# Cross attention with 64-dim heads: reciprocals spread as three bf16 rows, the output projection ahead of the next spread

## The reference, cut to what matters

```python
def _L1_xattn_ref(x, context, Wq, Wk, Wv, Wout, bout):
    HEADS, DIM_HEAD = 8, 64
    SCALE = DIM_HEAD ** (-0.5)
    b, n, _ = x.shape                 # 32, 128, 128
    m = context.shape[1]              # 128 (width 96)
    q = (x @ Wq).reshape(b, n, HEADS, DIM_HEAD)
    k = (context @ Wk).reshape(b, m, HEADS, DIM_HEAD)
    v = (context @ Wv).reshape(b, m, HEADS, DIM_HEAD)
    sim = jnp.einsum('bihd,bjhd->bhij', q, k) * SCALE
    attn = jax.nn.softmax(sim, axis=-1)
    out = jnp.einsum('bhij,bjhd->bihd', attn, v).reshape(b, n, HEADS * DIM_HEAD)
    return out @ Wout + bout
...
x = _layernorm(x + _L1_xattn_ref(x, ctx_768, ...), axis=-1)
```

## Time and profile before

| | us |
|---|---|
| median of 3 runs | 3455.29 (3452.86 to 3456.10) |
| the profiled execution | 3453.05 |
| its span in the trace | 3451.3 |
| the stage of the change, about | 1157 to 1449 in the span |
| PE / PEld / DVE / ACT / POOL busy | 80% / 57% / 57% / 40% / 37% |

### The profile page before, as it was taken

How to read it: one execution, slowest core, us unless ns; L and a number is a source line. 1 busy time by engine, 2 the same in 40 slices (tenths; PEclk the granted TensorE clock), 3 DMA queues, 4 the chain that set the end, 5 groups by cost and what they waited for, 6 DMA issues and landing times. The chain is left out here.

```text
span 3451.3 us, 78570 instructions
## 1 busy us (share of the span) xinstructions
PE 2777.9 (80%) x31785; PEld 1976.5 (57%) x31785; DVE 1960.1 (57%) x5133; ACT 1387.4 (40%) x3112; POOL 1272.5 (37%) x1365
## 2 busy tenths in 40 slices
PE   6980466577667699799899996798979999988986
PEld 3550233265443477556699985566456666665665
DVE  5987988406456344366554444464755555544665
ACT  3540455416334455344422222454133434334554
POOL 3440243317221111345323333453743333324555
PEclk9995677659678899899899998898999999998998
DMA  3000000030000000000000000001000000000000
GB/s 99 3 2 2 1 1 1 1 107 1 1 6 1 32 2 2 39 3 3 8 1 1 1 1 1 17 2 42 0 5 2 2 2 2 2 2 8 2 2 25
DMA packets 24454, 37.29 MB, mean 11 GB/s; under 512 B 569, under 2 KB 21185, under 8 KB 23233
## 3 DMA queue, kind: packets, MB, share of 16 engines
q1 hardware_dynamic: 24096, 32.30, 2.9%
HBM read 30.07 MB, written 2.23 MB: 9 GB/s over the span
## 5 line engine op out<-in xcount | busy, mean ns | idle before, releaser
L1193 POOL TENSOR_TENSOR L_attn__qk<-L_attn__turned 128x512 f32<-128x512 f32 x128 | 161.5, 1273 | 352.7 <-DVE L_attn__turned L1302 352.7
L4218 PE MATMUL psum<-L_ffn__e_hT,weights 128*128 128x256 f32 x1024 | 244.4, 382 | 0.0
L777 DVE TENSOR_REDUCE L_xattn__nm<-psum 128x8 bf16<-128x1024 f32 x128 | 156.4, 1224 | 149.4 <-PE psum L970 143.0
L1302 DVE TENSOR_TENSOR L_attn__turned<-psum,weights 128x1024 f32<-128x1024 f32 x128 | 153.4, 1219 | 144.7 <-PE psum L1409 141.7
L4218 PEld LDWEIGHTS psum<-L_ffn__e_hT,weights 128*128 128x128 f32 x1024 | 186.5, 192 | 20.5
L4072 DVE TENSOR_TENSOR L_ffn__e_a<-L_ffn__e_sg,psum 128x512 f32<-128x512 f32 x128 | 87.9, 687 | 176.2 <-ACT L_ffn__e_sg L4064 176.2
L4064 ACT ACTIVATE L_ffn__e_sg<-psum 128x512 f32<-128x512 f32 x128 | 76.5, 598 | 258.4 <-PE psum L4218 258.4
L717 ACT ACTIVATE L_xattn__pT<-psum 128x1024 f32<-128x1024 f32 x128 | 124.0, 1021 | 59.0 <-PE psum L998 59.0
L4231 PEld LDWEIGHTS psum<-weights,L_ffn__e_a 128*128 128x128 f32 x1024 | 134.4, 191 | 7.2 <-DVE L_ffn__e_a L4072 0.7
L1409 PE MATMUL psum<-L_attn__xT,weights 128*128 128x256 f32 x512 | 136.2, 399 | 1.9 <-DVE L_attn__turned L1302 1.2
L4231 PE MATMUL psum<-weights,L_ffn__e_a 128*128 128x128 f32 x1024 | 135.0, 275 | 0.5 <-DVE L_ffn__e_a L4072 0.5
(11 more groups left out here) (677 smaller groups left out, 7613.3 us busy)
## 6 DMA issues: line engine op xcount, KB each, us to landing
L_xattn__toeplitz<-s4d_kernel SPq DMA_DIRECT2D x8, 1024.0 KB, 5.7
weights<-pack SPq DMA_DIRECT2D x1, 3328.0 KB, 10.5
weights<-pack SPq DMA_DIRECT2D x1, 3140.0 KB, 10.5
weights<-pack SPq DMA_DIRECT2D x1, 2370.0 KB, 9.2
out_dram<-X SPq DMA_DIRECT2D x1, 2048.0 KB, 8.7
weights<-pack SPq DMA_DIRECT2D x1, 1732.5 KB, 10.3
ctxT<-ctxT_in SPq DMA_DIRECT2D x1, 1536.0 KB, 22.0
weights<-pack SPq DMA_DIRECT2D x1, 1376.0 KB, 5.5
```

The source lines that it names most:

```text
L777: nc.vector.tensor_reduce(nm[:, n % 2, :].rearrange("p (g c) -> p g c", g=4)[:, 2 * u:2 * u + 2, 0:4], scores[u].rearrange("p g (i q) -> p ...
L1193: nc.gpsimd.tensor_tensor(qk[:, p % 2, u], turned[:, g % 2, :, 0:2 * P], turned[:, g % 2, :, 2 * P:4 * P], ALU.add).then_inc(qk_sb, 1)
L1302: nc.vector.tensor_tensor(turned[:, g % 2], proj[u % 2].unsqueeze(1).to_broadcast([P, 2, 4 * P]), k.w(name + "rope").rearrange("p (t q) -> ...
L4218: last = nc.tensor.matmul(bank[g % 2][:, 256 * c:256 * c + 256], k.w(name + w)[:, o:o + P], hT, start=True, stop=True)
```

## The change

The reciprocal is no longer spread as one f32 row per head but as three bf16 rows that add up to it. The rows of C that `weigh` fills come in groups of 32, and each group holds several copies of its denominators, in rows that repeat every two. `spread2` now selects three of these copies, and DVE makes them different: the first holds the value rounded to bf16, the second the rounded remainder, the third the remainder of that. The columns `part_of_row` say which rows subtract. That takes five more DVE operations, each waiting for the one before, and `parts` has two buffers. PE's four matmuls read bf16 on both sides; the constant is cast to bf16 at the stage's start, and PE waits for that. `project_out(n - 1)` comes before `spread(n)`, behind a new wait for the reciprocal (inv_sb), as the reciprocal reads the bank C that the output is written to.

```diff
-    return (p == D64 * half + 32 * (c // 2) + c % 2).astype(np.float32).reshape(P, -1)
+    first = D64 * half + 32 * (c // 2) + c % 2
+    return ((p == first) | (p == first + 2) | (p == first + 4)).astype(np.float32).reshape(P, -1)
+def part_of_row():
+    part = np.arange(P) % 32 // 2
+    return np.stack([np.where(part == 0, 0.0, -1.0), np.where(part == 2, -1.0, 0.0)], 1).astype(np.float32)
...
                 def inverted(n):
                     dve.wait_ge(den_ps, n + 1)
-                    if n >= 1:
-                        dve.wait_ge(over_ps, n)
-                    nc.vector.reciprocal(rd[:], C[:, 0:P]).then_inc(rd_sb, 1)
+                    nc.vector.reciprocal(rd[:], C[:, 0:P]).then_inc(inv_sb, 1)
+                    dve.wait_ge(inv_sb, n + 1)
+                    nc.vector.tensor_copy(hi[:], rd[:]).then_inc(hi_sb, 1)
+                    dve.wait_ge(hi_sb, n + 1)
+                    nc.vector.scalar_tensor_tensor(out=less_hi[:], in0=hi[:], scalar=not_hi, in1=rd[:], op0=ALU.mult,
+                                                   op1=ALU.add).then_inc(less_hi_sb, 1)
+                    dve.wait_ge(less_hi_sb, n + 1)
+                    nc.vector.tensor_copy(himid[:], less_hi[:]).then_inc(himid_sb, 1)
+                    dve.wait_ge(himid_sb, n + 1)
+                    nc.vector.scalar_tensor_tensor(out=less_mid[:], in0=himid[:], scalar=is_lo, in1=less_hi[:],
+                                                   op0=ALU.mult, op1=ALU.add).then_inc(less_mid_sb, 1)
+                    dve.wait_ge(less_mid_sb, n + 1)
+                    if n >= 2:
+                        dve.wait_ge(over_ps, n - 1)
+                    nc.vector.tensor_copy(parts[:, n % 2, :], less_mid[:]).then_inc(rd_sb, 1)
...
                 dve.wait_ge(k.loaded[stage], 16)
+                nc.vector.tensor_copy(spread16[:], k.w(name + "spread2")).then_inc(spread16_sb, 1)
...
-                        last = nc.tensor.matmul(scores[n % 2][:, 1, P * c:P * c + P], spread2[:, P * c:P * c + P], rd[:],
+                        last = nc.tensor.matmul(scores[n % 2][:, 1, P * c:P * c + P], spread16[:, P * c:P * c + P], parts[:, n % 2, :],
...
                 pe.wait_ge(k.ctx_loaded, 16)
+                pe.wait_ge(spread16_sb, 1)
...
-                    spread(n)
                     if more and n % 2 == 0:
                         project(p + 1, 3)
                     if n >= 1:
+                        pe.wait_ge(inv_sb, n + 1)
                         project_out(n - 1)
+                    spread(n)
                     if n % 2 == 1 and p + 2 <= LAST:
                         turn_x(p + 2)
```

More of the change, by code:

```diff
@@ L230, in host_pack @@
     put(4, n + "spread2", spread2())
+    put(4, n + "part_of_row", part_of_row())
     n = "L1_ffn_"
@@ L1590, in attention64_cross @@
         sums2 = k.w(name + "sums2")
-        spread2 = k.w(name + "spread2")
+        spread16 = sb("spread16", [P, C2 * P], BF16)
+        hi, himid, parts = sb("hi", [P, P], BF16), sb("himid", [P, P], BF16), sb("parts", [P, 2, P], BF16)
+        less_hi, less_mid = sb("less_hi", [P, P]), sb("less_mid", [P, P])
+        not_hi, is_lo = k.w(name + "part_of_row")[:, 0:1], k.w(name + "part_of_row")[:, 1:2]
         scores = [k.psum[:, 4 + 2 * r:6 + 2 * r, :] for r in range(2)]
@@ L1607, in attention64_cross @@
         var_eps, rstd_sb, x_out = event("ln_var_eps"), event("ln_rstd"), event("x_out")
+        inv_sb, hi_sb, less_hi_sb, himid_sb, less_mid_sb, spread16_sb = (
+            event(n) for n in ("inv_sb", "hi_sb", "less_hi_sb", "himid_sb", "less_mid_sb", "spread16_sb"))
         with nc.Block() as block:
```

## The result

In 15 runs each the changed kernel took 3463.36 us in the median (3454.50 to 3465.61) and the kernel before 3455.29 (3450.29 to 3457.37): ratio 1.0023, 95% interval 1.0016 to 1.0030. In a second set (11 and 27 runs) it was 3459.34 against 3455.43, ratio 1.0018 (1.0009 to 1.0027). So the change costs 3 to 10 us, where 2.75 were forecast.

The account below looks back on a forecast made before the run. PE seemed the bound (busy 232.72 of 240 us), but ACT's queue was taken to gate its saving. Terms +1.4, +0.45, -0.2, +0.8 and +0.3 gave +2.75 us: 3458.0, range 3449 to 3466, its own 3453 to 3463.

Parts of the forecast that it names:

- Spread on PE: PE's spread matmuls: 1.00 us falls to 0.30 (bounds 0.22 and 0.39), saving 0.70 a step.
- The split on DVE: Three casts and two scalar_tensor_tensor behind each reciprocal on DVE: 1.50 us, bounds 1.3 and 1.9.
- rival (b): Split on DVE so short that it hides behind the output block: about 3450 us; chance 0.05.
- rival (c): Parts and spread cost more, POOL contention on DVE possible, each step pays: up to 3473, mostly near 3464; chance 0.22.
- The new order: Output before spread: even steps keep 0.08 of 0.93 us because ACT's queue waits, odd steps lose 0.18.
- rival (a): PE's saving carries into the next step, ACT's queue not the gate: -0.75 us a pair, 3445; chance 0.10.
- start: Cast of spread2 at the stage's start, 0.42 us, of which PE sees about 0.3.
- up to L1848 of step 1: Step 0 has no output block, so spread waits for its parts: +0.45 us.
- pairs and late steps: 14 pairs cost +1.4 us; two late steps without x transpose or projections gain 0.1 each.
- behind the last L1848: Last sequence has no cover: spread eviction 1.50 later less the 0.70 of spread, +0.8 us.
- Rival (d): PE, standing 1.3 us more in a pair, loses its clock; price like the slower-parts rival's; chance 0.03.
- The sum: Whole kernel +2.75 us, from a median of 3455.29 to 3458.0; chance 0.60.

Follow-up runs that it names:

- both handovers: Changed kernel with ACT evicting last projection and x before the spread, PE transposing x before waiting for parts: 3439.55 against 3455.43 before, ratio 0.9959.
- second trace: Trace of the changed kernel run again without an edit: median 3459.34 against 3455.43 for the kernel before, ratio 1.0018.
- first trace: First trace of the changed kernel, its execution 3465.61 us; median of that set 3463.36 against 3455.29 for the kernel before, ratio 1.0023.
- the control with the two columns: Kernel before with only the unused part_of_row columns added to the packed weights: median 3454.91, ratio 0.9996 to before.

## Why the prediction was right, and where it was off

**Spread on PE.** Taken at 0.30 us; it takes 0.23 (1402.66 to 1402.89), at the lower bound. The eviction starts 0.43 after its first matmul (0.50 was taken). The Trainium skill, "TensorE: Matmul & The Clock Gate", section "Back-to-back issue gap", gives 81 ns for each matmul of 128 columns in a stream of weight loads and matmuls. Four would take 0.32 us, an estimate from that page; the trace's 0.23 is less.

**The split on DVE.** Taken at 1.50 us from the reciprocal's end; it takes 1.55 (1410.34 to 1411.89). The combining steps were right (0.35), the casts 0.23 instead of 0.21: the line through 256 and 512 columns doesn't reach down to 128. The 0.77 us estimated from the Trainium skill's "VectorE: DVE Perf Modes" and rival (b) are out. POOL's contention of rival (c) did not come, as the groups of the changed kernel show (busy, mean ns):

```profile
L1750 DVE SCALAR_TENSOR_TENSOR L_xattn__less_mid<-L_xattn__himid,weights,L_xattn__less_hi 128x128 f32<-128x128 bf16 x32 | 11.2, 352 | 1.1
L1745 DVE SCALAR_TENSOR_TENSOR L_xattn__less_hi<-L_xattn__hi,weights,L_xattn__rd 128x128 f32<-128x128 bf16 x32 | 11.2, 351 | 1.1
...
L1755 DVE CAST L_xattn__parts<-L_xattn__less_mid 128x128 bf16<-128x128 f32 x32 | 7.2, 227 | 1.1
```

**The new order.** This is the step on which the forecast stood, and its sum held to 0.1 us: 0.96 won in even steps and 1.04 lost in odd ones, a pair 0.08 longer where 0.10 was forecast. The even saving turned up as L1848's wait of 0.69 for ACT (0.7 to 0.9 forecast), the odd step's as 0.40 to 0.59 for the parts and 0.74 for the x eviction (0.47 before). For the even side ACT's order alone brought 0.55 us a pair back, and both handovers together 1.38 of the 2.00 that stood in these waits and savings. The order alone with the f32 spread has the same two waits for ACT. So this queue, and not PE's work, is the gate of the even saving; rival (a) was wrong for that reason. In odd steps the parts are a second one, worth 0.58, as the kernel with two parts shows.

**The ends of the stage.** The prediction's terms against both traces, in us over before (start: from SP's load to the first matmul; pairs: from L1848 of step 1 to the last L1848):

| | forecast | second trace | first trace |
|---|---|---|---|
| start | 0.3 | 0.55 | 0.55 |
| up to L1848 of step 1 | 0.45 | 0.20 | 1.68 |
| pairs and late steps | 1.4 - 0.2 | 0.98 | 0.95 |
| behind the last L1848 | 0.8 | 0.96 | 1.77 |
| sum | 2.75 | 2.69 | 4.95 |

In the second trace every term is right to about 0.25, and that the sum is right to 0.06 is luck: PE waits for all of the cast of spread2, which takes 0.55 there and not the 0.42 of its row (it takes 0.42 in the run that makes it later), and step 0 costs less than taken. Of the 1.77 in the first trace 0.81 come before the last output starts, just the 0.8 of the forecast, and 0.96 from it on.

In the first trace a term was missing, the clock at the two ends, 2.26 by the difference between the traces. Rival (d) gave a lower clock 0.03, on the ground of a stretch where PE was busy 12 of 17 us and kept its clock. The changed kernel did keep it in all the pairs; what a fall at one of the ends would cost was not worked out, and the sum had nothing for it. How real (d) is, the split in the old order shows.

**The sum.** The stage is +2.69 us in one trace and +4.95 in the other, against +2.75. The medians say +8.07 and +3.9, with intervals of 5.5 to 10.4 and 3.1 to 9.3. The one trace's stage falls just below both, the other's is inside the second and just under the first. 0.4 to 0.5 us more lie in the end of the program. What fills the rest is open: the slots stage took 253.0 to 258.1 us at the same code, the control with the two columns shows no cost of theirs, and moving one cast took off more than its trace can show. 3463.36 is inside the range of 3449 to 3466, but 5.36 above the forecast of 3458 and 0.36 outside its own range of 3453 to 3463, which had 0.60; the first set's 1.0023 lies just outside "within 0.2%", on the side that had 0.20. The second set's 3459.34 is inside both. So the mechanism of the pairs was right, and the cost of the whole kernel was forecast too low, by 1 to 5 us.

## What to carry to other kernels

When one engine's work shrinks, follow each buffer's handover to the next engine's queue before the saving is counted: here the 0.96 us that PE saved in each even step went into waiting for an eviction that stood behind three others, and moving one call on ACT and one on PE turned +0.2% into -0.4%. A cheaper operation with a longer latency paid here only once the queue behind it let others pass: the split was worth 0.98 us a pair then. And a wait put into every step can have a second price beside its length, PE's clock, as the split in the old order shows.

## What the runs showed of the hardware that I had not expected

With two waits of 1.58 us in 19 us PE's granted clock fell again and again (mean 0.91 over 220 us), and 16 matmuls that took 1.16 us took 2.08; with waits of 0.4, 0.69 and 0.74 us in a pair of 17.44 us it stayed at 1.00. At the stage's end one wait of 1.70 us was followed by an output of 1.13 us behind the f32 spread (two traces) and of 1.25 to 2.05 behind the split's (eight). Four 16-bit 128x128 matmuls, each with its own weights, took 0.23 us together until the next block started, where eight records of f32 took 1.00. The same cast of 128x512 took 0.55 us at the stage's start and 0.42 behind the first maxima. And the wait for the parts cost PE what the weight loads' row says, 0.59, not PE's own 0.40: taking it away gave 0.58.
